# Layer 1's dense work in six pieces, and GpSimd's gather of that layer without pauses for landing

## The reference

```
x = x + gru(segment_sum(h[src] + relvectors[edge_type], dst), h)      h = layernorm(x)     layer 0
x = x + shared_mlp(layernorm(x)) + top-2 of 4 small experts           layer 0
x = x + segment_sum((layernorm(x) @ W.T + b)[src], dst) / (deg + 1)   layer 1
x = x + top-2 of 8 experts, 256 -> 1024 -> 256 with gelu              layer 1
```

## Time and profile before

| | |
|---|---|
| median of 3 runs | 3396.59 us (3394.66 to 3401.94) |
| profiled execution, its own time | 3414.43 us |
| its span, first to last instruction | 3412.9 us |
| mean granted TensorE clock | 0.772 |
| PE, DVE, ACT, POOL busy | 68%, 45%, 24%, 56% of the span |
| layer 1's graph pass, first gather to the experts' stage | 1529.9 to 2742.4 us |

### The profile page before, as it was taken

The page is one execution under the profiler, slowest core; times in us unless marked ns, Lnnn a source line. Parts: engine busy times, 40 slices in busy tenths (PEclk is TensorE's granted clock), DMA queues, the critical chain, the costliest instruction groups (busy, mean ns, idle before and its releaser), DMA issues. The chain is left out here.

```text
span 3412.9 us, 47179 instructions
## 1 busy us (share of the span) xinstructions
PE 2328.8 (68%) x11708; PEld 1564.6 (46%) x11709; DVE 1532.5 (45%) x4138; ACT 828.9 (24%) x1644; POOL 1923.9 (56%) x2043
## 2 busy tenths in 40 slices
PE   1478999988866775345666555444443389999996
PEld 1245555555443442132333232221111179999996
DVE  7445555555542433123555443332321156666663
ACT  2233333333322211020110000000000035555543
POOL 0364445556666666626666666666666445555553
PEclk6589999999986776566777766665665589999998
DMA  5322222223232323223333333333333443333334
GB/s 166 88 81 67 71 65 79 79 81 89 87 90 81 87 82 88 82 66 90 101 92 99 92 92 95 90 91 92 91 99 89 138 99 72 73 73 71 71 48 106
DMA packets 163077, 298.23 MB, mean 87 GB/s; under 512 B 47543, under 2 KB 106656, under 8 KB 162752
## 3 DMA queue, kind: packets, MB, share of 16 engines
q0 software_dynamic: 96736, 235.19, 26.3%
q1 hardware_dynamic: 41476, 39.54, 3.7%
q10 hardware_dynamic: 24732, 22.06, 2.1%
HBM read 255.78 MB, written 47.27 MB: 89 GB/s over the span
## 5 line engine op out<-in xcount | busy, mean ns | idle before, releaser
L763 POOL DMA_INDIRECT rows<-table,srcT x1568 | 1552.4, 990 | 985.5 <-issue 498.3
L829 PE MATMUL bank<-rows,onehot 128*128 x1952 | 672.7, 486 | 704.4 <-POOLq L751 435.6
L829 PEld LDWEIGHTS bank<-rows,onehot 128*128 x1952 | 218.6, 112 | 1118.8 <-issue 995.6
L789 DVE SCALAR_TENSOR_TENSOR onehot<-iota_row,tbase,dstT 128x512 f16 x488 | 366.6, 753 | 677.8 <-issue 429.2
L1923 ACT ACTIVATE hid<-bank,b 128x256 f32<-128x256 f32 x432 | 178.9, 465 | 291.5 <-PE bank L1875 266.6
L1873 PE MATMUL bank<-W_high,hid_high 128*128 128x256 f32 x864 | 244.9, 283 | 0.0
L1873 PE MATMUL bank<-xe_high,W_high 128*128 128x256 f32 x864 | 241.2, 279 | 4.8 <-DVE xe_low L1956 4.7
L1874 PE MATMUL bank<-xe_low,W_high 128*128 128x256 f32 x864 | 240.0, 278 | 0.0
L1875 PE MATMUL bank<-xe_high,W_low 128*128 128x256 f32 x864 | 240.0, 278 | 0.0
L1874 PE MATMUL bank<-W_low,hid_high 128*128 128x256 f32 x864 | 239.9, 278 | 0.0
L1875 PE MATMUL bank<-W_high,hid_low 128*128 128x256 f32 x864 | 239.9, 278 | 0.0
(11 more groups left out here) (351 smaller groups left out, 3754.0 us busy)
## 6 DMA issues: line engine op xcount, KB each, us to landing
rows<-table,srcT POOLq DMA_INDIRECT x1568
W<-in_L_ffn_W_dram SPq DMA_DIRECT2D x14, 1024.0 KB
x_res<-in_x_dram SPq DMA_DIRECT2D x1, 6144.0 KB, 22.4
normal<-xn ACTq DMA_DIRECT2D x11, 528.0 KB
table<-part ACTq DMA_DIRECT2D x11, 512.0 KB
totals<-x_res SPq DMA_DIRECT2D x11, 512.0 KB, 6.8
table<-part SPq DMA_DIRECT2D x6, 512.0 KB, 2.9
table<-part_b SPq DMA_DIRECT2D x6, 512.0 KB, 2.9
```

The source lines that it names most:

```text
L763: nc.gpsimd.indirect_dma_start(out=rows[:, k % (M * U), 0:ROW], out_offset=None, in_=q.table, in_offset=bass.IndirectOffsetOnAxis(srcT[:, ...
L789: last = nc.vector.scalar_tensor_tensor(onehot[:, ds(slot, U), :], iota_row[:, :].unsqueeze(1).to_broadcast([P, U, P]), base, dstT[:, ds(k ...
L829: last = nc.tensor.matmul(acc[:, 0:ROW], hots[:, ds(hot0 + s * P, P)], ring_rows[:, ds(row0 + s * ROW, ROW)], start=False, stop=False, ski ...
```

## The change

Steps `e0` to `e3` are cut into six pieces: `sums`, `gcn`, `turn`, `logits`, `rank`, `list` on PE, with `hots` split from `rank` on DVE. `run_layer1` takes the place of `run_graph` in layer 1 and places each piece behind another window, up to three groups later. The bodies of the pieces are as before. `pool_chunks` is called with `run = BLOCKS`, so POOL never stops at a run's end and each block is declared at the second DMA of the next. In the last group a PSUM bank is reused after two windows, and the wait there is adapted. DVE's chain semaphore is split in two.

```
@@ pe_windows
-                pe.wait_ge(q.evacuated, t + 1 - GW)
+                pe.wait_ge(q.evacuated, t + 1 - (GW // 2 if isinstance(g, int) and g == LAST else GW))
@@ PE's steps, cut where they waited for another engine
-        def pe_e0(pe, g, w):
+        def pe_sums(pe, g, w):
             pe.wait_ge(q2.evacuated, first_window(g) + w)
...
             last.then_inc(R["sumsT_ps"], 1)
+
+        def pe_gcn(pe, g, w):
             pe.wait_ge(R["sumsT_sb"], g + 1)
...
-        def pe_e1(pe, g, w):
-            n = w * P
+        def pe_turn(pe, g, w):
             pe.wait_ge(R["xn_ready"], g + 1)
...
             last.then_inc(R["xnT_ps"], 1)
+
+        def pe_logits(pe, g, w):
             pe.wait_ge(R["xnT_sb"], g + 1)
...
-        def pe_e2(pe, g, w):
+        def pe_rank(pe, g, w):
...
-        def pe_e3(pe, g, w):
+        def pe_list(pe, g, w):
@@ DVE: e1 is norm, e2 is route, e3 is rank and hots
-            chain.end()
+        def run_layer1(gather, stages):
+            def step(g, *names):
+                for name, back in names:
+                    if g - back >= 0 and name in stages:
+                        stages[name](g - back, size(g - back))
+
+            gather(0, 0)
+            for g in range(1, LAST):
+                step(g, ("logits", 2), ("list", 3))
+                gather(g, 0)
+                step(g, ("sums", 1), ("rank", 2))
+                if size(g) == GW:
+                    gather(g, 1)
+                step(g, ("gcn", 1))
+                gather(g, 2 if size(g) == GW else 1)
+                step(g, ("turn", 1), ("hots", 2))
+                if size(g) == GW:
+                    gather(g, 3)
+            step(LAST, ("logits", 2), ("list", 3))
+            gather(LAST, 0)
+            step(LAST, ("sums", 1), ("rank", 2), ("gcn", 1), ("hots", 2), ("turn", 1), ("list", 2))
+            step(LAST, ("logits", 1), ("rank", 1), ("hots", 1), ("list", 1))
+            gather(LAST, 1)
+            step(LAST, ("sums", 0), ("gcn", 0), ("turn", 0), ("logits", 0), ("rank", 0), ("hots", 0), ("list", 0))
@@ POOL
-                pool_chunks(pool, q2, 3)
+                pool_chunks(pool, q2, BLOCKS)
@@ the pieces by engine
+                           {"sums": pe_sums, "gcn": pe_gcn, "turn": pe_turn, "logits": pe_logits, "rank": pe_rank, "list": pe_list}
+                           {"sums": act_sums, "gcn": act_std, "turn": act_turn, "logits": act_exp, "rank": act_store}
+                norm, route = Chain(dve, "layer1_norm", 8), Chain(dve, "layer1_route", 64)
+                           {"gcn": dve_norm, "logits": dve_route, "rank": dve_rank, "hots": dve_hots}
```

More of the change, by code:

```diff
@@ L1525, in pe_e3, with act_sums @@
                                  skip_group_check=True).then_inc(R["listed"], 1)
-        def act_e0(act, g, w):
+        def act_sums(act, g, w):
             act.wait_ge(R["sumsT_ps"], g + 1)
@@ L1531, in act_e0, with act_std, act_turn @@
             last.then_inc(R["sumsT_sb"], 1)
+        def act_std(act, g, w):
             ln_sqrt(act, R["var"], R["std"], g, w)
-        def act_e1(act, g, w):
+        def act_turn(act, g, w):
             n = w * P
@@ L1539, in act_e1, with act_exp, act_store @@
             last.then_inc(R["xnT_sb"], 1)
+        def act_exp(act, g, w):
             act.wait_ge(R["lg_ready"], g + 1)
             nc.scalar.activation(f1["ex"][:, 0:w, :], f1["lg"][:, 0:w, :], ACT.Exp).then_inc(R["ex_ready"], 1)
-        def act_e3(act, g, w):
+        def act_store(act, g, w):
             act.wait_ge(R["xn_ready"], g + 1)
@@ L1547, in act_e3, with dve_norm @@
                           xn[:, 0:w, :]).then_inc(R["xn_out"], 16)
-        def dve_e1(dve, chain, g, w):
+        def dve_norm(dve, chain, g, w):
             if isinstance(g, int) and g == 0:
@@ L1574, in dve_e1, with dve_route @@
             ln_apply(first_tile(g), w, xn[:, :, 0:D]).then_inc(R["xn_ready"], 1)
-        def dve_e2(dve, chain, g, w):
+            chain.end()
+        def dve_route(dve, chain, g, w):
+            chain.begin(g)
             dve.wait_ge(R["logit_ps"], g + 1)
@@ L1592, in dve_e2, with dve_rank @@
             nc.vector.tensor_tensor(xn[:, 0:w, D:NROW], gate1, gate2, ALU.add).then_inc(R["gates_ready"], 1)
-        def dve_e3(dve, chain, g, w):
+        def dve_rank(dve, chain, g, w):
             eq = [f1[k][:, 0:w, :] for k in ("eq1", "eq2")]
@@ L1612, in dve_e3, with dve_hots @@
                                                       ALU.mult, ALU.add))
+            chain.end()
+        def dve_hots(dve, g, w):
             if isinstance(g, int) and g == 0:
@@ L1663, in _ @@
                 pe.sem_inc(q2.used, MH)
-                steps = [lambda g, w: pe_e0(pe, g, w), lambda g, w: pe_e1(pe, g, w), lambda g, w: pe_e2(pe, g, w), lambda g, w: pe_e3(pe, g, w), nothing]
-                run_graph(lambda g, i: pe_windows(pe, q2, g, i, BANKS2), steps, pe)
+                run_layer1(lambda g, i: pe_windows(pe, q2, g, i, BANKS2),
+                           {"sums": lambda g, w: pe_sums(pe, g, w), "gcn": lambda g, w: pe_gcn(pe, g, w),
+                            "turn": lambda g, w: pe_turn(pe, g, w), "logits": lambda g, w: pe_logits(pe, g, w),
+                            "rank": lambda g, w: pe_rank(pe, g, w), "list": lambda g, w: pe_list(pe, g, w)})
             @block.scalar
@@ L1673, in _ @@
                 act_split(act, 0, 0)
-                run_graph(lambda g, i: act_high_out(act, g, i), [lambda g, w: act_e0(act, g, w), lambda g, w: act_e1(act, g, w),
-                                              nothing, lambda g, w: act_e3(act, g, w), nothing], act)
+                run_layer1(lambda g, i: act_high_out(act, g, i),
+                           {"sums": lambda g, w: act_sums(act, g, w), "gcn": lambda g, w: act_std(act, g, w),
+                            "turn": lambda g, w: act_turn(act, g, w), "logits": lambda g, w: act_exp(act, g, w),
+                            "rank": lambda g, w: act_store(act, g, w)})
                 act.wait_ge(R["xn_out"], 16 * (LAST + 1))
@@ L1691, in _ @@
                 start.link(nc.vector.tensor_copy(spare_to[:, :], to_list[:, :]))
-                chain = Chain(dve, "layer1_chain", 64)
-                run_graph(dve_gather(dve, q2, evacuate2),
-                          [lambda g, w, f=f: f(dve, chain, g, w) for f in (dve_e1, dve_e2, dve_e3)] + [nothing, nothing], dve)
+                norm, route = Chain(dve, "layer1_norm", 8), Chain(dve, "layer1_route", 64)
+                run_layer1(dve_gather(dve, q2, evacuate2),
+                           {"gcn": lambda g, w: dve_norm(dve, norm, g, w), "logits": lambda g, w: dve_route(dve, route, g, w),
+                            "rank": lambda g, w: dve_rank(dve, route, g, w), "hots": lambda g, w: dve_hots(dve, g, w)})
                 rows_i, tiles_i = lists[0:1, 0:E1], lists[0:1, E1:2 * E1]
```

## The result

The changed kernel takes 3245.5 us (median of 4 runs, 3239.2 to 3246.8), where the kernel before took 3395.6 (4 runs, 3389.6 to 3401.9): ratio 0.9549, 95% interval 0.9534 to 0.9564, so 153 us less by the ratio, 148 to 158; the two medians stand 150 apart. Measured again later it was 0.9551 (0.9538 to 0.9564). The forecast was 138 us less. Direction and mechanism held; the size was 12 to 15 us short. The median of 3245.5, and 3243.4 by the ratio (0.9549 x 3396.6), are outside the forecast's own bounds of 3247 to 3268 and just inside its wider range of 3243 to 3290.

What follows compares the result with a forecast made beforehand. POOL's 784 gather DMAs were taken to bound layer 1's graph pass. Terms 1 to 5 summed as -148 + 1 + 2 + 4 + 3 = -138 us, from 3396.6 to 3258.6 us; forecast 3247 to 3268, wider range 3243 to 3290.

Steps and rivals of the forecast that it cites:

- Term 1: POOL's gather in layer 1: 65 pauses at ends of three-block runs go, 2.28 us each, 148 us off POOL's chain.
- Term 2: Layer 1's gather: landing checked two DMAs later, margin 0.15 to 0.2 us; 1.5 more waits, 1 us added.
- The landing rival: Layer 1's gather: the landing wait comes back at every block; 78 us at 0.4 us a block, so 3337; chance 0.07.
- Term 3: Layer 1's gather instructions: a denser POOL meets more of DVE's work, 0 to 4 us added, taken as 2.
- Term 4: Layer 1's early groups with the six pieces: DVE's work plus waits exceed POOL's 47 us; 4 us lost.
- the VectorE rival: Layer 1's early groups: DVE takes over at 53 us in seven groups, costing 27 us, about 3282; chance 0.24.
- The closing ring of waits: First window's emptying: DVE waits for ACT, ACT for PE, PE for DVE; slower than before, 3489 us; chance 0.03.
- Term 5: Layer 1's last two windows: more PE work between them, 33 us, delays the shared block's slot; 3 us of stall.
- more than the sum, 150 us or more: Whole kernel: gain of 150 us or more, only if terms 2 to 5 are all nothing; chance 0.06.

## Why the prediction was right, and where it fell short

**The bound** was right: a flat POOL, pauses in its chain, and the whole gain in that chain.

**Term 1, 148 us, was mis-sized by 5.** The step: 175.3 / 68 = 2.58 us for a pause. The 68 contain 3 short waits of another kind; the 65 pauses alone are 2.67 us, and the row of one (2.65) was already nearer. 65 x 2.36 = 153, measured 153.4. I divided a row by a count that mixed two kinds, and had the better figure in rows 4.

**Term 2, 1 us**: 3 by the profile. The margin, 0.14 us rather than 0.15 to 0.2, holds for 186 of 195 blocks, and the two runs with that question moved show both sides of it. The landing rival is wrong. The estimate of 2.3 us from the Trainium skill's "DMA: Bandwidth & Descriptors", section "Anatomy of one DMA", is 0.4 us below the row: POOL started again 2.67 us after its last DMA's instruction. The measurement decides, and it still leaves 0.14 us (2.81 less 2.67).

**Term 3, 2 us**: no loss; the 784 instructions took 4 us less, 771.8 for 775.8, of which 2.4 are a median of 0.946 us for 0.949; in a second execution of the changed kernel they took 774.2. The step that failed is the scaling with POOL's busy share. The long ones are nearly all gathers that begin behind a two-input VectorE instruction, and the number of those instructions did not change: 195 meetings with a one-hot, before 209. Of the Trainium skill's "SBUF — State Buffer" I had taken the rule on two-port modes from "SBUF: two separate sides"; it would have cost 2 us, and the total shows no such cost. Gathers behind TENSOR_SCALAR instructions did wait; whether those ran in such a mode no trace tells. The section "Who interferes with whom" of that same page of the Trainium skill has the rule that fits the runs: a VectorE instruction with two SBUF inputs contends with a GpSimd instruction that reads SBUF, and here the gather reads its indices there. The Trainium skill's page also says, in "SBUF: two separate sides", that the one which comes second is held for the other's whole instruction, and the traces agree for the gather: it ends 0.82 us after the VectorE instruction that it began behind, in 88 of 88 cases. Beside short adds of 0.42 us this is a loss of 0.07 us on average and 0.24 at most, beside the 2048 columns of L1444 it was 1.40. The other way round nothing shows: the 392 adds took 0.41 to 0.45 us, all of them.

**Term 4, 4 us, and the VectorE rival (0.24)**: nothing came. My 46 us of VectorE work for a group of 9 blocks was some 5 too high: 41.0 measured in the changed kernel (1616 to 1665 us, 49 us less 8.0 of waits), 40.4 with the pauses alone gone. What failed more is what I did next: I added waits of 3 to 7 us to the work and called the sum its need. Waits give way when the engine becomes the late one. With eight adds a window VectorE worked 54 us of a group's 55, with waits of about 1. Its need is its work alone, and that was below GpSimd's 47. The right comparison left 6 us of room, not 2 to 6 us of lack, with 19 us of lead in the ring on top. The closing ring of waits, the rival for slower, had the same fault: nothing of it in any run.

**Term 5, 3 us**: 4.0, at the place and for the reason given: PE stood 33.8 us between the two windows (2388.6 to 2422.3), where the forecast had 33. A second execution had 2.6. The list moved takes it away.

**The rival "more than the sum, 150 us or more" (0.06)** is what happened, though not on its condition that terms 2 to 5 all be nothing. Against the forecast term 1 gave 5 us more, term 3 6 and term 4 4, small waits at a block's second DMA 2; term 2 took 2 and term 5 1: 14 in all. Term 3's part is partly spread between executions, 774.2 us when the changed kernel ran again.

## What to carry to other kernels

Where one engine's chain sets the time, price each pause from rows of that pause alone, not from a total over a count that mixes kinds. For an engine that is not yet the bound, compare its work, without its waits, with the bound's need for the same stretch; waits are the slack, and with a ring between the two they vanish before they cost. A producer that must know when its own transfer landed can ask late enough that its next issues cover it; here one issue too early cost 218 us, and one later brought 6.

A short mean can hide a long wait: look at where the long instructions begin before calling a contention small.

## What the hardware showed that I had not expected

GpSimd's indirect DMA instruction (128 rows, indices in SBUF) takes 0.94 to 0.96 us when no VectorE instruction runs beside it, in all 339 such cases of the changed kernel. When it begins at least 0.10 us after a VectorE instruction that reads two SBUF tiles, it ends 0.82 us after that instruction's end: 1520 of 1523 cases in fourteen traces, with loss up to 1.4 us behind a 2.28 us instruction of the changed kernel. As means this is 0.13 us beside the 128x512 one-hot and 0.07 beside 128x256 adds. An instruction of equal length whose second input is in PSUM, and `bn_stats` with its one input, leave it at 0.95; TENSOR_SCALAR from SBUF to SBUF holds it too (81 of 89). Eight adds a window, which nobody waited for, lengthened the gather's instructions by 19 to 21 us in all, against the two executions of the changed kernel; eight `bn_stats` of the same length by 2.5 to 5, of which 2.4 are the median of 0.949 in place of 0.946.
